# A one-core decoder layer: transposes of x1 and of the cross output one head on, first-layer chunks in pairs, cross value groups one head on

## What is computed

```python
x = layernorm(x + self_attention(x))        # x1: q, k RMS-normed, rotary, causal softmax, projection
x = layernorm(x + cross_attention(x, ctx))  # x2: q from x1, k and v from ctx, causal softmax, projection
x = layernorm(x + ffn(x))                   # x3: light and heavy feed-forward of the RMS-normed x2, exact gelu
```

## Time and profile before

| what | value |
|---|---|
| median of 3 runs | 1015.32 us (1014.58 to 1018.68) |
| the profiled execution's own time | 1012.79 us |
| its span, first to last instruction | 1011.1 us |
| PE busy | 918.6 us, 91% |
| DVE busy | 734.0 us, 73% |
| ACT busy | 489.9 us, 48% |
| POOL busy | 468.7 us, 46% |
| mean granted clock of TensorE | 0.965 of 2.4 GHz |
| chain of work that ended last | PE 63%, DVE 17%, issue 9%, POOL 5%, ACT 3% |

### The profile page before, as it was taken

One profiled execution on the slowest core, in us unless ns is written; L12 is line 12 of the kernel. 1 busy time (PEld: TensorE's weight loads), 2 busy tenths in 40 slices (PEclk: granted clock), 3 DMA queues, 4 the chain that ended last, 5 costly groups with the idle time before them and its releaser, 6 DMA issues.

```text
span 1011.1 us, 21587 instructions
## 1 busy us (share of the span) xinstructions
PE 918.6 (91%) x7776; PEld 707.6 (70%) x7776; DVE 734.0 (73%) x1843; ACT 489.9 (48%) x1047; POOL 468.7 (46%) x883
## 2 busy tenths in 40 slices
PE   2577988999999999999999999999999999998896
PEld 2445565787878787777868787777878786766675
DVE  8668578787778778887777788787777788563612
ACT  1131444546364545546374655556464645445343
POOL 2264464635464554736355555636354554233221
PEclk8659899999999999999999999999999999999999
DMA  3819191917556481917456472909365462805100
GB/s 106 172 41 132 31 119 34 117 34 99 71 75 87 61 109 33 116 36 108 62 77 95 58 102 41 120 23 117 53 90 81 65 86 51 109 13 62 24 1 22
DMA packets 79643, 74.22 MB, mean 73 GB/s; under 512 B 8592, under 2 KB 78896, under 8 KB 79536
## 3 DMA queue, kind: packets, MB, share of 16 engines
q1 hardware_dynamic: 75872, 68.90, 48.9%
q10 hardware_dynamic: 3664, 3.94, 1.2%
HBM read 17.49 MB, written 4.20 MB: 21 GB/s over the span
## 4 chain that ended last, share of the span: by engine, by line
PE 63%; DVE 17%; issue 9%; POOL 5%; ACT 3%; DMA 0%; POOLq 0%; ACTq 0%; DVEq 0%
PE bank L342 58%; PE bank L367 4%; DVE mx L871 3%; POOL pr L1177 3%; ACT pr L728 2%; DVE x L948 2%; DVE y L920 1%; DVE st L927 1%; DVE rest L855 1%; DVE ss L973 1%; DVE on L911 1%; DVE nat2q L860 1%; ACT sq L817 1%; DVE nt L990 1%; DVE rden L908 1%
## 5 line engine op out<-in xcount | busy, mean ns | idle before, releaser
L728 ACT ACTIVATE pr<-bank 128x384 f32<-128x384 f32 x512 | 242.4, 499 | 209.0 <-PE bank L342 208.7
L871 DVE TENSOR_REDUCE mx<-bank 128x3 f32<-128x384 f32 x512 | 268.1, 551 | 89.0 <-PE bank L342 87.0
L1177 POOL TENSOR_SCALAR_AFFINE_SELECT pr<-pr 128x256 f32<-128x256 f32 x512 | 227.9, 453 | 215.6 <-ACT pr L728 211.4
L342 PE MATMUL bank<-w,g 128*128 128x256 f32 x576 | 170.8, 389 | 1.1 <-ACT g L740 1.1
L342 PE MATMUL bank<-cmaskb,idb 128*128 128x256 bf16 x512 | 144.5, 282 | 17.2 <-DVE mx L871 7.5
L740 ACT ACTIVATE g<-bank,b 128x256 f32<-128x256 f32 x144 | 68.3, 475 | 111.4 <-PE bank L342 110.9
L1201 POOL TENSOR_TENSOR xTlow<-xT,xThigh 128x512 fp32r<-128x512 f32 x16 | 21.2, 1322 | 173.0 <-ACT xThigh L674 173.0
L342 PEld LDWEIGHTS bank<-w,g 128*128 128x128 f32 x576 | 89.6, 190 | 5.2 <-ACT g L740 1.5
L342 PE MATMUL bank<-stk1k,stk1q 97*128 97x128 bf16 (+1 forms) x512 | 86.6, 255 | 0.0
L342 PE MATMUL bank<-stk1q,stk1k 100*128 100x256 bf16 (+1 forms) x512 | 80.6, 256 | 4.4 <-DMA stk1q<-mT 3.3
L342 PE MATMUL bank<-stk2k,stk2q 97*128 97x128 bf16 (+1 forms) x512 | 82.3, 246 | 0.0
(11 more groups left out here) (143 smaller groups left out, 1800.6 us busy)
## 6 DMA issues: line engine op xcount, KB each, us to landing
stk1q<-nat1q SPq DMA_DIRECT2D x96, 128.0 KB, 4.6
stk1k<-nat1k SPq DMA_DIRECT2D x96, 128.0 KB, 6.5
stk2k<-nat2k SPq DMA_DIRECT2D x96, 128.0 KB, 4.6
stk2q<-nat2q SPq DMA_DIRECT2D x96, 128.0 KB, 6.2
xT<-in_xT SPq DMA_DIRECT2D x16, 256.0 KB, 7.8
x<-in_x SPq DMA_DIRECT2D x16, 256.0 KB, 6.9
ctxT<-in_ctxT SPq DMA_DIRECT2D x16, 256.0 KB, 2.7
out_x<-x SPq DMA_DIRECT2D x16, 256.0 KB, 6.7
```

The lines of the kernel that those rows point to most:

```text
L342: return nc.tensor.matmul(out, lhsT, rhs, start=start, stop=stop, skip_group_check=check)
L728: nc.scalar.activation(pr[:, h % (2 * HG), :], ring_bank("T", a, b, h)[:, 0:3 * P], ACT.Exp, scale=HD ** -0.5)\
L871: V.tensor_reduce(mx3[:, h, :], scored[:, 0:3 * P].rearrange("p (k t) -> p k t", k=3), AX.X, ALU.max, negate=True).then_inc(s_mx[a], 1)
L1177: G.affine_select(out=slot, in_=slot, compare_op=ALU.is_ge, fill=0.0, base=0, pattern=[[0, 2], [1, P]], channel_multiplier=-1).then_inc(s_ ...
```

## The change

Only constants of the lists change, and one of them becomes a pair, so that the self and the cross value groups have offsets of their own.

```diff
-                        add(HG * gr + VALUES_AFTER, values, 1, s, gr)
+                        add(HG * gr + VALUES_AFTER[1], values, 1, s, gr)
...
-                        add(HG * gr + VALUES_AFTER, values, 2, c, gr)
+                        add(HG * gr + VALUES_AFTER[2], values, 2, c, gr)
...
-VALUES_AFTER = 7
-X1T_AT, OUT2_AT, Q2_AT = 1, (3, 5, 10, 12), 4
-HIDDEN_AT = (6, 7, 8, 10, 11, 13, 14, 15, 16)
+VALUES_AFTER = (None, 7, 8)
+X1T_AT, OUT2_AT, Q2_AT = 2, (3, 5, 11, 14), 4
+HIDDEN_AT = (6, 6, 8, 8, 10, 10, 12, 12, 15)
...
-COPY2_AT, COPY_XN_AT, COPY_V1_AT = 4, 13, 15
+COPY2_AT, COPY_XN_AT, COPY_V1_AT = 6, 13, 15
...
-QN_AT, NORM2_AT, SPLITQ_AT, RESID2_AT, MAXT_AT, STAT2_AT = (1, 2), 7, 5, 1, 3, 6
+QN_AT, NORM2_AT, SPLITQ_AT, RESID2_AT, MAXT_AT, STAT2_AT = (1, 2), 6, 5, 1, 3, 6
```

## The result

| | before | changed |
|---|---|---|
| median of 7 runs each, us | 1015.32 (1013.2 to 1019.58) | 1027.12 (1022.56 to 1027.93) |
| ratio, 95% interval | | 1.0102 (1.0084 to 1.012) |
| profiled execution: time, span, us | 1012.79, 1011.1 | 1027.12, 1025.4 |
| a steady step, us | 56.40 | 57.42 |

The account below looks back on a forecast made before the run. PE was taken as the bound, busy 55.06 of each 56.40 us step. Terms 12.3 + 0 - 1.9 = +10.4 us gave 1023.2 from the profiled execution, 1025.7 from the median; forecast 1025 us, range 1010 to 1030.

Parts of the forecast that it names:

- Part 1: T2, cross value groups one head on: 0.80 us lost in each of steps 1 to 13, +12.3 us in all.
- Part 2: S1, transposes of x1 one head on: a head fills 0.28 of 0.56 us lost; their start stays tied to DVE.
- Part 3: S1, cross transposes later, division earlier, chunks paired: 0.76 us wait goes, new wait at h9 0.34 (0 to 0.34).
- Part 4: Last chunk ahead of h15: h15 to h4 of S2 stays DVE's 3.81 us; PE waits 0.72 at h3 and h4.
- Parts 2 to 4: S1 and start of S2: together 0, lower bound -0.34 us a step, or -3.7 us in 11 steps.
- Part 5: The drain: fewer waits for the cross output and for masks, -1.9 us, from 0 to -3.2.
- A: S2 start not bound by DVE, so 0.72 us is hidden: +2.5, about 1018 us; chance 0.14 together with D.
- B: T2 wait for the cross output doesn't come: 1010 to 1013 us, near 1002 with A; chance 0.11.
- C: Third group, last of T2, delays x1T's copy and S1's last group: up to +6.5 us, 1032; chance 0.07.
- D: Nothing happens, PE's list being bound by its own matmuls: 1015 us; chance 0.14 together with A.

Follow-up runs that it names:

- division at 7: The changed kernel with DVE's division of the cross output back ahead of head 7's maximum: 1022.35 us, ratio 1.0055 to the kernel before.
- groups undone: The changed kernel with all three cross value groups back at slots 7, 11, 15: 1015.51 us, ratio 1.0005.
- x1 alone: The kernel before with only the transposes of x1 one head on (slot 2): 1012.86 us, ratio 0.9978.
- groups alone: The kernel before with only the first three cross value groups of T2 one head on (slots 8, 12, 16): 1035.89 us, ratio 1.0196.
- group ahead: The changed kernel with the first cross group at slot 8 issued ahead of that slot's self transposes, others at 12 and 16: 1014.27 us, ratio 0.9994.

## Why the prediction was right, and where it was off

**Part 1 (the groups): right in place and sign, short in size.** 0.80 was foreseen, 0.96 measured in steps 3 to 13. The term of the group itself is 0.89 (0.63 to 1.52), just above the upper bound of 0.88, and not 0.80. The 0.09 between the transposes and a group exist too (530.36 to 530.95 is 0.59, where four transposes and a head are 0.49). The other 0.07 is x1, later against the projection, which I had put at 0. In steps 14 and 15, 0.95 was foreseen and 0.56 and 0.50 came. The failed step is the root of x1: I had head 12's exponential later by 0.17. From the self projection to the transposes of x1 it took 6.51 us before and 6.06 in step 14 after (860.79 to 867.30, 878.01 to 884.07). h11 goes ahead of the second group now, its exponential is done while the group runs, and the one of head 12 comes sooner.

**Part 2 (x1): right.** The wait fell from 0.40 to 0.22, the transposes stayed tied to DVE, and alone the move is worth 0.03 us a step.

**Part 3 (S1): right, the term at h9 mis-sized.** 0.34 was foreseen, as the upper end of its range; h9 came at 9.28 and could have come at 8.82 (the run with the division at 7), so 0.46. The maximum of h5, behind the split of q, did not start 0.28 sooner, at 6.82, but at 6.97 (547.50 - 540.53): the cast took 0.57 in place of 0.43. I had allowed for contention only as a gain. By the Trainium skill (SBUF — State Buffer, "Who interferes with whom") a cast can enter a two-port mode and take the shared port pair as an exclusive lock, and the side that starts first has it for its whole instruction. The traces agree: 0.43 us when the cast is 0.05 ahead of POOL's addition, 0.99 when the addition is first, with POOL's addition at 0.97 or 0.72 in turn. Where the cast begins 0.2 us or more ahead of an addition's end, it ends 0.28 to 0.31 us behind that end, whenever it began. In these rows the blocking is a little short of whole instructions: behind the addition the cast needs 0.3 us and not its shortest 0.43, and an addition held up by the cast ends some 0.12 us before the cast's end plus 0.72.

**Part 4 (h15 to h4): right to the hundredth,** 3.81 us. The waits at h3 and h4 are 0.55 by the rows, and by starts the 0.7 foreseen: from h2 to h4 of S2 it is 2.09 us in step 9, and it was 1.37 before. The bound was seen from both sides by moving the chunk and by moving the residual. What was missing was its condition, that h14's maximum be over.

**Parts 2 to 4 together:** 0 foreseen, +0.06 measured between x1 and h4.

**Part 5 (the drain): right in sign, short in size, and close in part by luck.** From the transposes of x1 in step 16 to the end it is 88.40 us before (1011.1 - 922.70) and 85.43 after (1025.4 - 939.97): -3.0 in place of -1.9, inside the bound of -3.2. The start of S2 came only 0.8 sooner and not 1.1, since it now waits 0.47 us for the loading of the q stack, a wait that I hadn't seen. In the kernel with the groups undone that wait is 1.16 us, and the start of S2 is only 0.1 sooner than before. From the start of S2 to the last value group 1.6 was won, double what I took. Nearly all of that lies in T2 of step 16; the kernel before, then the changed one:

```profile
954.49:966.19 11.70, 9.22 (x80) 4.16 (x80) 3.07 (x9) 7.38 (x19) 7.00 (x18) 0.71 0.07 23
```

```profile
970.95:981.11 10.16, 8.13 (x81) 3.85 (x81) 3.13 (x9) 7.49 (x19) 7.03 (x18) 0.83 0.08 27
```

PE stood still for 0.45 us less, and was busy for 1.09 less with the same matmuls, at a granted clock of 0.83 in place of 0.71. At a clock near 0.83 the same stretch took 10.96 us with x1 alone and 10.14 with the groups alone; at 0.68 to 0.71 it took 11.47 to 11.70 in the three kernels with the first group at 7, and 10.53 to 10.81 in four with it at 8. So some 0.8 us goes with the groups, as I had it, and the rest with the clock of these executions. Behind the last value group another 0.6 was won, but that stretch took 44.3 to 46.2 us in the eleven kernels, whatever was moved. A third of the 2.1 us of mask waits is also 0.7 and not 0.8.

**The sum.** Foreseen +10.4; the two medians are 11.8 apart, the ratio gives 10.4 (8.5 to 12.2). In the profiled executions the span grew by 14.3: 0.40 up to x1 of step 1, 1.60 and 2.85 in the next two, 11.36 in the eleven up to step 14, 0.56 and 0.50, less 2.97 in the drain. Against the forecast the steady steps are 2.6 over (11.36 for 11 times 0.80), the early ones 3.2 over (4.85 for 1.6), steps 14 and 15 are 0.8 under (1.06 for 1.9) and the drain 1.1 under. So the profiled executions differ by 3.9 more than was foreseen, and the medians by 1.4 more. That the total came this close is partly luck: terms off in both directions, and a profiled execution of the kernel before that was a fast one. Of the early steps some 2.4 us (1.60 + 2.85 less two times 1.03) had no term at all; the last section has them.

**Rivals.** A fell: the 3.81 us are bound by DVE. B fell at the point that was named for it: `on` came 3.19 us behind the start of the split, not earlier. C did not happen: with the third group last in T2, x1T and the last group are on time. D is no case, since the time moved.

## What to carry to other kernels

In this kernel PE is busy 98% of a step, and other engines arrive within hundredths of a microsecond of it, at places where the list of waits shows nothing. Before moving work from in front of a waiting instruction, look at when its input was ready: if that is as late as PE is, the work was free there and costs its whole length anywhere else. A time saved early in a phase counts only if no other engine's chain ties the phase's end, so measure the longest such chain in two kinds of steps and fill it with PE work from both sides.

## What the runs showed of the hardware that was not expected

**An 0.06 us shift decides about half a microsecond.** The same cast of 128x512 took 0.43, 0.54, 0.57, 0.66 and 0.99 us in five kernels, repeated in each steady step within 0.02, by where it met POOL's two additions. Where the cast runs into an addition, starting it sooner buys nothing: it ends 0.3 us behind the addition.

**The clock in step 2.** The first steps lack the feed-forward, and PE waits for DVE in them. In the changed kernel's profile PE waited 1.74 and 1.26 us for maxima in S1 of step 2, and in the columns below the granted clock falls to 0.72 and 0.69 of 2.4 GHz over stretches of 10 us, which is part of the time at the lower level, 1.2 GHz. Changed kernel, then the kernel before (PEclk is the third number from the end):

```profile
150.00:160.00 10.00, 9.29 (x53) 7.29 (x52) 6.27 (x17) 1.77 (x4) 1.57 (x3) 0.72 0.51 63
...
170.00:180.00 10.00, 10.00 (x88) 5.99 (x87) 6.52 (x15) 6.34 (x16) 5.90 (x14) 0.69 0.06 17
```

```profile
150.00:160.00 10.00, 8.89 (x57) 6.51 (x56) 7.15 (x21) 1.08 (x2) 0.00 (x0) 0.91 0.37 49
...
170.00:180.00 10.00, 8.73 (x93) 6.35 (x94) 4.89 (x10) 6.49 (x16) 5.56 (x13) 1.00 0.45 66
```

The kernel with the groups undone has 0.83 and 1.00 in the same stretches, the one with the group ahead 1.00 and 1.00. The waits by themselves don't decide it: with the group ahead PE also waited 1.74 and 1.26 us for the same maxima of step 2, at a granted clock of 1.00, and its steps 1 and 2 took 102.8 us together where the changed kernel's took 106.9. These are single executions, so how much of the 2.4 us the change itself causes, and how much differs from one execution to the next, stays open.
